# Two-layer graph attention on one core: instance operands loaded in twelve pieces and results stored in four, in place of whole transfers

## The reference

```python
def _gat_layer(h, mask, b):
    scores = jnp.einsum('...nd,...md->...nm', h, h)
    scores = jnp.where(mask, scores, NEG)
    attn = jax.nn.softmax(scores, axis=-1)
    return jnp.einsum('...nm,...md->...nd', attn, h) + b
...
h = jnp.einsum('bnc,hdc->bhnd', x, Wh)          # 4 heads
out_h = _gat_layer(h, mask[None, None], bh[None, :, None, :])
cat = jnp.transpose(out_h, (0, 2, 1, 3)).reshape(B, N, H * D)
z = jax.nn.leaky_relu(cat, negative_slope=0.2)
h2 = jnp.einsum('bnk,dk->bnd', z, Wo)
out2 = _gat_layer(h2, mask[None], bo)
z2 = jax.nn.leaky_relu(out2, negative_slope=0.2)
...  # layer norm of z2 over D, then layer norm of x + that
```

## Time and profile before

| | |
|---|---|
| median of 3 runs | 3214.2 us (3212.13 to 3216.12) |
| the profiled execution | 3214.32 us, of which the span of the trace is 3212.5 us |
| layer 1, instances 1 to 30 | 411.69 to 2389.18 us of the span, 1977.49 us |
| layer 2, instances 33 to 38 | 2655.87 to 3056.19 us, 400.32 us |
| projections, masks and norms | what is left |

### The profile page before, as it was taken

How to read it: one execution, slowest core, us unless ns; L and a number is a source line. 1 busy time by engine, 2 the same in 40 slices (tenths; PEclk the granted TensorE clock), 3 DMA queues, 4 the chain that set the end, 5 groups by cost and what they waited for, 6 DMA issues and landing times. The chain is left out here.

```text
span 3212.5 us, 124648 instructions
## 1 busy us (share of the span) xinstructions
PE 2952.8 (92%) x49473; PEld 2176.3 (68%) x49473; DVE 2695.4 (84%) x5576; ACT 2311.7 (72%) x2766; POOL 2534.0 (79%) x1431
## 2 busy tenths in 40 slices
PE   6868899999999999999999999999998789999980
PEld 4426577777777777777777777777766667777760
DVE  5675788888888888888888888989886469999987
ACT  2148677777777777777777777877776457777776
POOL 1138689889998998999999999989988069898980
PEclk8989999999999999999999999999999989999995
DMA  5208898998889988898889989998887868898863
GB/s 204 80 0 316 216 155 157 164 163 162 155 159 168 165 158 151 168 165 165 156 161 169 162 158 156 170 160 164 157 149 155 252 143 155 160 164 161 157 125 96
DMA packets 1442508, 514.20 MB, mean 160 GB/s; under 512 B 1359054, under 2 KB 1416844, under 8 KB 1439884
## 3 DMA queue, kind: packets, MB, share of 16 engines
q1 hardware_dynamic: 1442060, 507.32, 80.7%
HBM read 105.27 MB, written 66.06 MB: 53 GB/s over the span
## 5 line engine op out<-in xcount | busy, mean ns | idle before, releaser
L547 POOL TENSOR_TENSOR low<-probs 128x1024 f16<-128x1024 f32 x1280 | 2395.4, 1893 | 396.8 <-ACT probs L824 291.2
L824 ACT ACTIVATE probs<-scores,shifted_max 128x2048 f32<-128x2048 f32 x640 | 1282.5, 2004 | 216.2 <-DVE shifted_max L1040 213.2
L689 PE MATMUL ps<-operands 128*128 128x512 f16 x2560 | 973.4, 380 | 7.3 <-DMA v_parts<-h_d 3.8
L690 PE MATMUL ps<-operands 128*128 128x512 f16 x2560 | 972.8, 380 | 0.0
L1035 DVE CUSTOM_DVE_ANT_0 scores<-ps,mask,neg_max 128x1024 f32<-128x1024 f32 x640 | 821.8, 1284 | 128.3 <-issue 86.4
L852 ACT COPY probsT<-ps 128x1024 bf16<-128x1024 bf16 x640 | 647.6, 1012 | 391.1 <-PE ps L698 386.0
L698 PEld LDWEIGHTS ps<-ident,probs 128*128 128x128 bf16 x10240 | 649.7, 98 | 375.9 <-issue 206.5
L1035 DVE CUSTOM_DVE_ANT_0 scores<-ps,mask 128x1024 f32<-128x1024 f32 x640 | 782.1, 1222 | 139.8 <-PE ps L690 131.1
L698 PE MATMUL ps<-ident,probs 128*128 128x128 bf16 x10240 | 780.4, 219 | 15.8 <-DVE probsT L1049 9.1
L708 PE MATMUL ps<-v_parts,probsT 128*128 128x64 f16 x10240 | 685.2, 193 | 3.8 <-ACT probsT L852 3.8
L709 PE MATMUL ps<-v_parts,probsT 128*128 128x64 f16 x10240 | 685.7, 193 | 1.5 <-issue 1.5
(11 more groups left out here) (142 smaller groups left out, 1818.5 us busy)
## 6 DMA issues: line engine op xcount, KB each, us to landing
operands<-hT_d SPq DMA_DIRECT2D x40, 512.0 KB, 4.7
operands<-hT_d SPq DMA_DIRECT2D x80, 256.0 KB, 4.2
v_parts<-h_d SPq DMA_DIRECT2D x40, 512.0 KB, 4.5
probsT<-low SPq DMA_TRANSPOSE x1280, 3.5
z_d<-outs SPq DMA_DIRECT2D x38, 512.0 KB, 3.5
scores<-in_adj SPq DMA_DIRECT2D x16, 1024.0 KB, 4.8
h_d<-probs SPq DMA_DIRECT2D x32, 512.0 KB, 5.3
hT_d<-probsT SPq DMA_DIRECT2D x32, 512.0 KB, 4.6
```

The source lines that it names most:

```text
L547: pool.tensor_tensor(low[:, u, w], probs[:, u, w], high[:, u, w], ALU.subtract).then_inc(sem(f"low{half}"), 1)
L689: pe.matmul(ps[:, b, :], hi_lo[:, p, t * P:(t + 1) * P], hi_lo[:, p, w], start=True, stop=False)
L690: scored = pe.matmul(ps[:, b, :], hi_lo[:, p, t * P:(t + 1) * P], lo_hi[:, p, w], start=False, stop=True)
L824: act.activation(probs[:, 1 - u, :], scores[:, 1 - u, :], ACT.Exp, bias=shifted_max[:, 1 - u:2 - u], scale=-1.0, accum_out=row_sum[:, held ...
```

## The change

- An instance's operands come in twelve DMAs of 128 KB: four for `hi_lo` (512 columns each), two for each half of rows of `lo_hi` (64 rows by 1024 columns), four for `v_parts`. One is issued per tile step, t = 4 to 15.
- The result is stored in four DMAs of 128 KB, one for each output group, at t = 0, 1, 3 and 7 of the next instance, each behind a wait for its own group.
- TensorE waits in t = 0 for 12 x 16 counts in place of 4 x 16; waits on `z_stored` count 64 for each result in place of 16.
- The loads ahead of each layer are 24 DMAs in place of 8, and the last result of layer 1 is stored in four.

```diff
-OPERAND_DMAS = 4
+OPERAND_DMAS = 12
...
             def load_part(i, parity, k):
 
                 s = sem(f"operands{parity}")
-                if k == 3:
-                    sp.dma_start(v_parts[:, parity, :], h_d[:, i, :] if isinstance(i, int) else h_d[:, bass.ds(i, 1), :]).then_inc(s, 16)
+                if k >= 8:
+                    w = slice((k - 8) * 4 * P, (k - 7) * 4 * P)
+                    sp.dma_start(v_parts[:, parity, w], h_d[:, i, w] if isinstance(i, int) else h_d[:, bass.ds(i, 1), w]).then_inc(s, 16)
                     return
-                to, row, at, rows_ = ((hi_lo, 0, 0, P), (lo_hi, 0, D, D), (lo_hi, D, 0, D))[k]
+                if k < 4:
+                    to, row, at, rows_, w = hi_lo, 0, 0, P, slice(k * N // 4, (k + 1) * N // 4)
+                else:
+                    to, row, at, rows_, w = lo_hi, (k - 4) // 2 * D, D - (k - 4) // 2 * D, D, slice(k % 2 * N // 2, (k % 2 + 1) * N // 2)
                 at = i * P + at
-                sp.dma_start(to[row:row + rows_, parity, :],
-                             hT_d[at:at + rows_, :] if isinstance(i, int) else hT_d[bass.ds(at, rows_), :]).then_inc(s, 16)
+                sp.dma_start(to[row:row + rows_, parity, w],
+                             hT_d[at:at + rows_, w] if isinstance(i, int) else hT_d[bass.ds(at, rows_), w]).then_inc(s, 16)
...
-            def store_z(i, p, base=0):
-                sp.wait_ge(sem("out_copied"), i * 4 + 4)
+            def store_z(i, p, k, base=0):
+                sp.wait_ge(sem("out_copied"), i * 4 + k + 1)
                 gate(sp, "sp")
-                sp.dma_start(z_d[:, i - base, :] if isinstance(i, int) else z_d[:, bass.ds(i - base, 1), :], outs[:, p, :]).then_inc(sem(f"z_stored{p}"), 16)
+                w = slice(k * 4 * D, (k + 1) * 4 * D)
+                sp.dma_start(z_d[:, i - base, w] if isinstance(i, int) else z_d[:, bass.ds(i - base, 1), w], outs[:, p, w]).then_inc(sem(f"z_stored{p}"), 16)
...
-                k = t - 3
+                k = t - 4
                 if 0 <= k < OPERAND_DMAS and not (isinstance(i, int) and i in (0, LAYER1 - 1, LAYER1, INSTANCES - 1)):
...
-                if t == 10 and not (isinstance(i, int) and i in (0, LAYER1, INSTANCES - 1)):
-                    store_z(i - 1, 1 - p, LAYER1 if second else 0)
+                if t in (0, 1, 3, 7) and not (isinstance(i, int) and i in (0, LAYER1, INSTANCES - 1, INSTANCES)):
+                    store_z(i - 1, 1 - p, (0, 1, 3, 7).index(t), LAYER1 if second else 0)
...
-            store_z(LAYER1 - 1, 1)
+            for k in range(4):
+                store_z(LAYER1 - 1, 1, k)
```

More of the change, by code:

```diff
@@ L409, in load_y @@
             def load_y(b):
-                sp.wait_ge(sem(f"z_stored{b % 2}"), 8 * (LAYER1 + b - b % 2) + 16)
+                sp.wait_ge(sem(f"z_stored{b % 2}"), 32 * (LAYER1 + b - b % 2) + 64)
                 sp.dma_start(y_of(b), z_d[:, b, :]).then_inc(sem(f"y_loaded{b}"), 16)
@@ L443, in _ @@
             for b in range(4):
-                sp.wait_ge(sem(f"z_stored{b % 2}"), 16 * (b // 2 + 1))
+                sp.wait_ge(sem(f"z_stored{b % 2}"), 64 * (b // 2 + 1))
             sp.wait_ge(sem("exp_done"), LAYER1 * NT)
@@ L452, in _ @@
             for u in range(2):
-                sp.wait_ge(sem(f"z_stored{u}"), 8 * LAYER1)
+                sp.wait_ge(sem(f"z_stored{u}"), 32 * LAYER1)
             quads(sp, p2_step)
@@ L833, in tile_step @@
                     if k == 0:
-                        since(act, sem(f"z_stored{held}"), (old - held) * 8)
+                        since(act, sem(f"z_stored{held}"), (old - held) * 32)
                     act.copy(z_halves(held, k, 0), by_tile(group_bank(k))).then_inc(sem("out_high"), 1)
@@ L1060, in tile_step @@
                         gate(dve, "dve")
-                        since(dve, sem(f"z_stored{held}"), (old - held) * 8)
+                        since(dve, sem(f"z_stored{held}"), (old - held) * 32)
                     gate(dve, "dve")
```

## The result

The changed kernel takes 3351.3 us at the median (3347.0 to 3379.8, 4 runs; a fifth on record took 3364.8) against 3214.0 (3212.1 to 3216.1), a ratio of 1.045 with a 95% interval of 1.040 to 1.050. The profiled execution was the slowest of the four: 3379.8 us with a span of 3377.9. The forecast was 3341.

The account below looks back on a forecast made before the run. The prediction took TensorE to bound the kernel: 3214.3 + 115 (stalls) + 27 (clock) + 10 (loads ahead) - 25 (late transposes) = 3341 us, 4.0% slower, chance 0.45; range for 8 in 10: 3285 to 3405 us.

Parts of the forecast that it names:

- TensorE bounds, and a stall isn't made good: Attention instances: TensorE sets the pace at 4.07 us a tile step, without idle time to catch up after a stall.
- the 68 to 70 forecast: Sign in the profile after: instances take 68 to 70 us in place of 65.9.
- The last load: TensorE's step 0 at 36 instance starts: stalls 3.2 us each for the last piece, +115 us (79 to 162).
- The estimate of 2.3 us by the fit: Landing of a 128 KB load: 2.0 us plus bytes over 436 GB/s; judged too short in this traffic.
- my lower bound of 2.1 us: Landing of the last piece: at least that of a 64 KB load on an idle queue, 2.1 us.
- SP falls behind: Rival, twelve load steps per instance: late SP makes TensorE wait for transposes, 86 us more, about 3427 us; chance 0.05.
- My 3.66 us of 4.07: SP's time per tile step with two transposes and a load: 3.66 us of 4.07, so the load fits.
- The clock, +27 us: TensorE after stalls: half the 36 followed by a half-clock stretch, 18 x 1.5 = +27 us (0 to 61).
- Loads ahead of the layers, +10 us: Before each layer: 24 DMAs in place of 8 take more SP time, +10 us (0 to 18).
- What is given back, -25 us: DMA queue within instances: smaller pieces delay transposes less, returning late-transpose waits, -25 us (-30 to -5).
- At nothing: SP's issue time, store waits, load waits for last instance's matmuls, and layer 1's final four stores: counted as no cost.
- The rival on the other side, that the last piece is in time: TensorE's step 0: last piece lands in time, only smoothing counts, 3199 us, 0.5% faster; chance 0.05.

Follow-up runs that it names:

- e8: Changed kernel plus 12 unread matmuls ahead of TensorE's operand wait in step 0, at the 18 even instance starts only: 3339.2 us, ratio 1.0391.
- e2: Changed kernel, loads still in steps 4 to 15, but v_parts counted on its own semaphore, awaited by TensorE in step 3: 3194.2 us, ratio 0.9944.
- e9: e2 with the operands of instances 0, 1, 32 and 33 loaded whole ahead of the layers (16 DMAs, not 48): 3192.2 us, ratio 0.9922.
- e1: Changed kernel with its twelve loads one tile step earlier, in steps 3 to 14: 3197.6 us, ratio 0.9952.
- e5: Changed kernel's twelve loads in steps 4 to 15, with the kernel before's whole store in step 10: 3381.7 us, ratio 1.0509.
- e6: Kernel before's whole loads in steps 3 to 6, with the changed kernel's four stores: 3235.0 us, ratio 1.0058.
- e7: e5 with its twelve loads one step earlier, in steps 3 to 14, store whole in step 10: 3206.8 us, ratio 0.9962.

## Why the prediction came out, point by point

- **TensorE bounds, and a stall isn't made good.** Right. The 165 us are in the two stretches, and no instance catches up; those of layer 1 take 70.6 us on average, a little over the 68 to 70 forecast.
- **The last load, +115 us.** The mechanism was right, and the sum nearly: 127.3 us in the profiled execution, 126.4 in the second one that was profiled, beside e8. Its two parts were off in opposite directions. The landing was forecast at 3.1 us and is 2.7 at the median for all `v_parts` pieces of layer 1; at the 36 starts it is 2.8 on average. The issue was forecast 0.1 us behind TensorE and is 0.6 behind it on average; the last 0.15 us, from the landing to the first matmul, the sum didn't have. That these set each other off was luck. The estimate of 2.3 us by the fit cited from the Trainium skill's page "DMA: Bandwidth & Descriptors" meets the landing at even starts (2.2, below), but not at odd ones (3.4) nor the average. The row behind my lower bound of 2.1 us wasn't on an idle queue, as I had it: SP issued other loads 0.6 us before it and 0.6 us after. The bound held even so, with 2.1 us as the least at the starts.
- **"SP falls behind" was priced apart, and is a part of the truth.** SP's waits in layer 1, before and then after:

```profile
SPq L157 <- POOL low L547: 322.6, 627, 1.2
```

```profile
SPq L157 <- PE ps L687: 144.4, 58, 4.2
SPq L157 <- POOL low L553: 109.7, 264, 1.1
```

Before, SP waited for GpSimd 627 times, which is to say that it was on time; after, 264 times, and it stands 144 us behind TensorE's stalls. My 3.66 us of 4.07 took a load's time on SP at its usual 0.4 us; the longest in layer 1 now held SP for 2.0 us. The lateness never starved TensorE of transposes (1.0 us in layer 1), so this rival's price of 86 us was wrong. It pushed back the last load instead, by half a microsecond.
- **The clock, +27 us: the term that was mis-sized.** Not half of the starts but 33 of 36 are followed by low clock (28 in the second execution). The half rested on the length of the gap, with 3.2 us between one of 2.90 and one of 3.73, and the length alone doesn't decide: in the changed kernel the clock fell at start 22 with a stall of 2.44 us and stayed up at start 23 with one of 3.28. Stretches of the changed kernel exceed those of e2, which has no stall, by 2543.0 - 2355.8 = 187.2 us, and the stalls are 127.3 of it; 60 us are left for the clock, against 27. TensorE's busy time in them says the same in another way: 2412.0 us against 2348.3 in e2 for the same matmuls, 63.7 more. That is 1.8 us for each of the 33 starts where I took 1.5, so it was mainly their number that failed. By the second execution it is 2528.7 - 2355.8 - 126.4 = 46.5 us, and by e8 36 to 43 us (36 x 1.0 to 1.2). The amount differs from run to run: the mean granted clock was 0.947 in the profiled execution, 0.952 in the second, and 0.955 to 0.957 in the three fastest on the first chip, so the 30 us between the slowest run and these go along with a lower clock. The page "TensorE: Matmul & The Clock Gate" of the Trainium skill, section "HAM oscillation", describes this pattern, and the traces agree, with low clock behind 33 and 28 of 36 waits for a DMA.
- **Loads ahead of the layers, +10 us.** Wrong in size: 0.2 us outside the stretches (834.9 against 834.7), in which layer 1 begins 2.6 us later and what follows the last stretch is 2.3 us shorter. In the second execution the same part took 828.2 us, so differences of a few us there say nothing; 10 us more are not seen in either, and e9 shows no gain from undoing it.
- **What is given back, -25 us.** Right: 22.0 us by e2's stretches, 16.0 by those of e1. TensorE's wait for transposes in layer 1 goes from 20.6 to 1.0 us.
- **At nothing.** The store's waits and its own issue showed no cost in the changed kernel: e5, without them, isn't faster. But that four stores are harmless holds only beside cut-up loads; e6 showed 0.6% in the other case, which I hadn't priced.

The sum as it came out, for the profiled execution: 127.3 (stalls) + 59.9 (clock) + 0.2 - 22.0 = 165.4 us, the clock's term being what is left over (63.7 by the busy time). For the second execution it is 126.4 + 46.5 - 6.5 - 22.0 = 144.4 us of its 144.5. The forecast of 3341 is within 10 us of the median, but 39 below the profiled execution: stalls 12, clock 33 and return 3 too low, loads ahead 10 too high. That it stands so near the median is in part luck. The rival on the other side, that the last piece is in time, was priced at 3199 us; e1 and e2, which put it in time, gave 3198 and 3194. The rule of the Trainium skill's page "DMA: Bandwidth & Descriptors", section "Rules for kernel authors", to coalesce small transfers, didn't decide here: e7 is 0.4% faster for having twelve loads where there were four.

## What to carry to other kernels

Spreading a load over a loop moves its last piece to the loop's end: compare the issue of the last piece, not of the first, with the first reader's wait, and count the landing in full if they coincide. A single count for all operands makes the earliest reader wait for the piece that is needed last; a count for `v_parts` alone cost two more semaphores here, one for each parity, and was worth 5 points (a ratio of 0.994 in place of 1.045). In this kernel, where TensorE bounds, stalls of 2.3 to 5 us once an instance cost about a third to a half more than their length, since the clock fell behind most of them.

## What the runs showed of the hardware

The landing of the last piece differs by the parity of the instance. At the 14 odd starts from 5 to 31 it took 3.0 to 4.1 us, at the 14 even starts from 4 to 30 2.1 to 2.4. The second execution has 3.0 to 3.9 and 2.1 to 2.3, as was expected before it ran. The DMA queues while that piece was in flight, at instance 13 and then at instance 14:

```profile
q8 instruction: 1, 0.02, 2.1%
...
v_parts<-h_d SPq DMA_DIRECT2D x1, 128.0 KB, 3.4
```

```profile
q1 hardware_dynamic: 992, 0.34, 65.2%
...
v_parts<-h_d SPq DMA_DIRECT2D x1, 128.0 KB, 2.2
```

At every one of the 14 odd starts one 16 KB packet of the instruction queue ran in this time, for 0.9 to 1.5 us, and at none of the even ones. The parity is not what matters, but the packet: in e1, with the loads one step earlier, a packet meets the last piece of the 14 even instances from 4 to 30, which then takes 2.8 to 4.0 us, and it meets none of the 14 odd instances from 5 to 31, whose last piece takes 2.1 to 2.7. I take these packets for the fetch of code (their place is shown, their purpose is inferred). They come along the whole loop, 18 of them between 1200 and 1340 us.

How one packet makes the piece 1.2 us late is shown in part. A DMA raises its semaphore in 16 counts. At starts 5, 23 and 27 only the last of them is late and the fifteenth came 2.2 to 2.5 us after the issue. At the other 11 all sixteen are late: the first came 3.0 us or more after the issue, where at even starts it came after 1.7 to 1.9. So in most cases it isn't one part of the piece that is held up but all of it. At these 11, 8 or more packets of 256 bytes, as the transposes ahead of the piece move them, still ended over 1.3 us after its issue, and at the other three and at the even starts none did. Whether the piece waits for these isn't shown. As one step of the loads moved the packet from one parity to the other, whether some place of the last piece meets none at all is an open question.
